# Attention of a gated cross-attention and mixture-of-experts layer: scores in pairs on two row strips, the row maximum as a bias, a new issue order

## The reference

```python
# x, ctx: 16 x 128 x 512 and 16 x 128 x 256; regrouped by 128 tokens
xn = (x - mean(x)) / sqrt(var(x) + 1e-5)
q = rope(xn @ Wq); k = rope(ctx @ Wk); v = ctx @ Wv          # 32 heads of 16
w = softmax(q @ k.T * 0.25, axis=-1)                          # per head, 128 x 128
x = x + tanh(g0) * ((w @ v) @ Wout + bout)
xn2 = (x - mean(x)) / sqrt(var(x) + 1e-5)
probs = softmax(xn2 @ gate_w.T); top 6
x = x + tanh(g1) * (sum over top 6 of probs * expert(xn2) + shared(xn2))
```

## Time and profile before

| | us |
|---|---|
| median of 3 runs | 1501.24 (1496.4 to 1513.0) |
| the profiled execution, its own time | 1500.2 |
| its span, first to last instruction | 1498.0 |

### The profile page before, as it was taken

One profiled execution on the slowest core, in us unless ns is written; L12 is line 12 of the kernel. 1 busy time (PEld: TensorE's weight loads), 2 busy tenths in 40 slices (PEclk: granted clock), 3 DMA queues, 4 the chain that ended last, 5 costly groups with the idle time before them and its releaser, 6 DMA issues.

```text
span 1498.0 us, 32482 instructions
## 1 busy us (share of the span) xinstructions
PE 1408.3 (94%) x8414; PEld 1187.6 (79%) x8415; DVE 839.9 (56%) x1682; ACT 499.7 (33%) x982; POOL 700.7 (47%) x1135
## 2 busy tenths in 40 slices
PE   4899999999999955999999999999999999999998
PEld 2566666666666644899999999999999999898987
DVE  4677777778777743444444444444444444256666
ACT  3344444445444411233333333333333333111111
POOL 3457754444544241548354555555555400745553
PEclk8799999999999856999999999999999999999999
DMA  5022323211321225534444444444443442356674
GB/s 190 18 92 76 134 92 134 75 75 75 119 105 65 79 108 178 168 100 141 144 141 144 141 144 141 143 143 143 143 143 107 122 143 86 104 166 202 206 206 138
DMA packets 146857, 190.03 MB, mean 127 GB/s; under 512 B 32531, under 2 KB 99604, under 8 KB 144116
## 3 DMA queue, kind: packets, MB, share of 16 engines
q1 hardware_dynamic: 125108, 99.31, 22.3%
q0 software_dynamic: 21696, 90.06, 17.5%
HBM read 116.80 MB, written 72.50 MB: 126 GB/s over the span
## 4 chain that ended last, share of the span: by engine, by line
PE 73%; DVE 13%; issue 5%; ACT 3%; SPq 2%; POOL 1%; DMA 1%; DVEq 0%; ACTq 0%; POOLq 0%
PE bank L1362 33%; PE bank L1396 18%; PE bank L616 8%; PE bank L641 5%; DVE smax L888 3%; PE bank L1373 3%; PE bank L654 2%; DVE soft L891 2%; PE bank L623 2%; PE bank L671 1%; ACT soft_t L533 1%; SPq L1183 1%; DVE x L937 1%; ACT soft L527 1%; DVE stats L940 1%
## 5 line engine op out<-in xcount | busy, mean ns | idle before, releaser
L1362 PE MATMUL bank<-w_hi,x_hi 128*128 (+1 forms) x1144 | 289.6, 334 | 21.0 <-DVE x_lo L1437 18.5
L1362 PE MATMUL bank<-w_hi,x_lo 128*128 (+1 forms) x1144 | 277.2, 323 | 0.0
L1362 PE MATMUL bank<-w_lo,x_hi 128*128 (+1 forms) x1144 | 276.9, 323 | 0.0
L205 POOL CAST w_hi<-w_raw 128x352 fp32r<-128x352 f32 x144 | 69.2, 531 | 379.2 <-PE bank L1362 379.2
L1453 DVE SCALAR_TENSOR_TENSOR act<-silu,row_w,bank 128x352 f32<-128x352 f32 x111 | 64.4, 580 | 301.2 <-ACT silu L1311 300.3
L1362 PEld LDWEIGHTS bank<-w_hi,x_hi 128*128 128x128 f32 x1144 | 193.0, 190 | 21.3 <-issue 18.6
L1311 ACT ACTIVATE silu<-bank 128x352 f32<-128x352 f32 x143 | 66.5, 465 | 402.7 <-PE bank L1362 402.7
L1362 PEld LDWEIGHTS bank<-w_lo,x_hi 128*128 128x128 f32 x1144 | 200.2, 189 | 0.0
L1362 PEld LDWEIGHTS bank<-w_hi,x_lo 128*128 128x128 f32 x1144 | 199.6, 189 | 0.0
L1396 PE MATMUL bank<-w_hi,a_hi 128*128 (+3 forms) x429 | 171.4, 400 | 7.6 <-DVE a_lo L1441 6.9
L1396 PE MATMUL bank<-w_lo,a_hi 128*128 (+3 forms) x429 | 169.7, 396 | 0.0
(11 more groups left out here) (183 smaller groups left out, 2316.8 us busy)
## 6 DMA issues: line engine op xcount, KB each, us to landing
xr<-expert_rows SPq DMA_DIRECT2D x444, 64.0 KB, 1.9
y_rows<-y SPq DMA_DIRECT2D x111, 256.0 KB, 2.0
w_raw<-in_w POOLq DMA_DIRECT2D x18, 1408.0 KB, 6.7
w_raw<-in_w POOLq DMA_DIRECT2D x18, 512.0 KB, 7.8
x_sb<-in_x SPq DMA_DIRECT2D x16, 256.0 KB, 3.0
x_res<-in_x SPq DMA_DIRECT2D x16, 256.0 KB, 3.9
x_rows<-x SPq DMA_DIRECT2D x16, 256.0 KB, 4.3
x_rows<-row SPq DMA_DIRECT2D x16, 256.0 KB, 4.4
```

The source lines that it names most:

```text
L205: nc.gpsimd.tensor_copy(w1_hi[d][half][:, s], w1_raw[:, d, halves[half]]).then_inc(w_hi_made, 1)
L1362: last = nc.tensor.matmul(to[:, 0:WIDTH], xx[jt][:, d, :], w[d][half][:, cols], start=(d == 0 and xx is x_hi and w is w1_hi), stop=(d == D ...
```

## The change

- PE issues the scores of two units together at even u, alternating between the two strips (`score_pair`), and waits for the exponentials of the unit just before (`exp_done` of u - 1 and older).
- DVE's maximum is written negated; the subtraction is gone. ACT reads the scores from PSUM and takes the exponential of each head with that maximum as the bias, four instructions per unit. The scale 0.25 moves into the masks of k (`C_EVEN`, `C_ODD`).
- The transposes of the rotated q go from u 4 to u 3 and of k from u 5 to u 4, with ACT's q_t copy from u 5 to u 3 and the k_t copies from u 5 to u 4.
- The output projection is issued in two halves, six matmuls at u 3 and six at u 4 behind the pair of scores. The addition of the bias and the residual go to u 5, the normalised row to u 7.
- `transpose_row` and `x2_hi` move to u 0 of PLACE, `c_hi` to u 0 and `c_lo` to u 1 of PROJECT, the router's chain from u 5 to u 3, the first statistics from u 2 to u 3, xn from u 6 to u 7. `rank` waits in addition for the projection to be read out of bank 1.
- SP issues the load of x before it waits for `c_lo`.
- `rsqrt` starts from a power of -0.5 on POOL and makes one Newton step instead of three.

```diff
@@ rsqrt, POOL
                 ch = Chain(pool, chain_sem, 2 + 3 * NEWTON, b)
+                if isinstance(b, int) and b == 0:
+                    pool.wait_ge(small_in, 16 * 5)
...
-                ch.step(g.tensor_scalar(y[:].bitcast(I32), vpos[:].bitcast(I32), -0.5, RSQRT_BITS, ALU.mult, ALU.add))
+                ch.step(g.tensor_tensor(y[:], vpos[:], const[:, C_HALF:C_HALF + 1], ALU.pow))
@@ attend, ACT
-                    act.wait_ge(shifted, b * GROUPS + u + 1)
-                    a.activation(soft[u % 2][:], soft[u % 2][:], ACT.Exp, scale=SCALE).then_inc(exp_done, 1)
+                    act.wait_ge(smax_done, b * GROUPS + u + 1)
+                    need(act, prob_mm, b * GROUPS + u - 1)
+                    for h in range(4):
+                        last = a.activation(soft[u % 2][:, h, :], bank[2 + u % 2][:, h * P:(h + 1) * P], ACT.Exp,
+                                            bias=smax[u % 2][:, h:h + 1])
+                    last.then_inc(exp_done, 1)
@@ score_pair, PE
-                    need(pe, shifted, b * GROUPS + u - 1)
+                    need(pe, exp_done, b * GROUPS + u)
                     for c in range(2):
+                        for w in (u, u + 1):
+                            r, ch = 32 * (w % 4), 2 * (w // 4) + c
+                            last = nc.tensor.matmul(bank[2 + w % 2][:, c * 2 * P:(c + 1) * 2 * P],
+                                                    q_t[j][r:r + 32, ch, :],
+                                                    k_t[j][r:r + 32, ch].rearrange("p e n -> p (e n)"),
+                                                    start=True, stop=True)
@@ one_round, PE
-                    scores(at, u)
...
+                    if u % 2 == 0:
+                        score_pair(at, u)
+                    if at(TAIL) and u == 4:
+                        project_out(1, *at(TAIL))
+                    if at(PROJECT) and u in (0, 4, 7):
+                        project(u, *at(PROJECT))
                         project_late(u, *at(PROJECT))
+                    if at(PLACE) and u == 0:
+                        transpose_row(*at(PLACE))
+                    probs(at, u)
+                    if at(TAIL) and u in (0, 2):
                         tail(u, *at(TAIL))
+                    if at(PROJECT) and u in (1, 2):
                         project(u, *at(PROJECT))
...
                     values(at, u)
+                    if at(PROJECT) and u == 3:
+                        project(u, *at(PROJECT))
                     if at(PLACE) and u == 6:
-                        rank(at(PLACE)[0])
+                        rank(at(PLACE)[0], at(TAIL))
                     if at(TAIL) and u == 3:
-                        project_out(*at(TAIL))
+                        project_out(0, *at(TAIL))
@@ attend, DVE
-                v.tensor_reduce(smax[u % 2][:], s3, AX.X, ALU.max).then_inc(smax_done, 1)
-                dve.wait_ge(smax_done, b * GROUPS + u + 1)
-                need(dve, prob_mm, b * GROUPS + u - 1)
-                v.tensor_tensor(soft[u % 2][:], s3, smax[u % 2][:, :, None].to_broadcast([P, 4, P]), ALU.subtract)\
-                    .then_inc(shifted, 1)
+                v.tensor_reduce(smax[u % 2][:], s3, AX.X, ALU.max, negate=True).then_inc(smax_done, 1)
@@ one_round, SP
                     waits_apart(sp, passed_sp, (xn_done, b - 1))
-                    waits_apart(sp, passed_sp, (c_lo_done, b))
                     if not (isinstance(b, int) and b == 0):
                         sp.dma_start(x_sb[j][:], x[b]).then_inc(x_in[j], 16)
+                    waits_apart(sp, passed_sp, (c_lo_done, b))
```

More of the change, by code:

```diff
@@ L563, in one_round @@
                     attend(at, u)
-                    if at(PROJECT) and u == 5:
+                    if at(PLACE) and u == 0:
+                        b = at(PLACE)[0]
+                        act.wait_ge(x2_mm, b + 1)
+                        need(act, gate_mm, b)
+                        a.activation(x2_hi[:].rearrange("p c n -> p (c n)"), bank[1][:], ACT.Copy)\
+                            .then_inc(x2_hi_done, 1)
+                    if at(PROJECT) and u == 0:
+                        b = at(PROJECT)[0]
+                        act.wait_ge(c_in, 16 * (b + 1))
+                        need(act, v_mm, b)
+                        a.activation(c_hi[:], c_raw[:], ACT.Copy).then_inc(c_hi_done, 1)
+                    if at(PROJECT) and u == 4:
                         b, j, n = at(PROJECT)
@@ L628, in _, with score_pair @@
             pe.wait_ge(ones_done, 2)
-            def scores(at, u):
+            def score_pair(at, u):
                 if at(ATTEND):
@@ L635, in scores @@
                         pe.wait_ge(kt_done, 2 * (b + 1))
-                    r = 32 * (u % 4)
-                    need(pe, shifted, b * GROUPS + u - 1)
+                    need(pe, exp_done, b * GROUPS + u)
                     for c in range(2):
[L640 to L645, removed]
+                        for w in (u, u + 1):
[4 more added lines that the diff above has]
+                                                    start=True, stop=True)
+                            if c == 1:
+                                last.then_inc(score_mm, 1)
             def probs(at, u):
@@ L717, in transpose_values, with project_out @@
                 four_transposes(bank[1], attn[:].rearrange("p h d -> p (h d)")).then_inc(at_mm, 1)
-            def project_out(b, j, n):
-                if isinstance(b, int) and b == 0:
-                    pe.wait_ge(w_lo_done, 3)
-                pe.wait_ge(at_lo_done, b + 1)
-                three(bank[1][:], at_parts, o_w, DC, lambda t, c: t[:, c, :], lambda w, c: w[:, c, :])\
-                    .then_inc(o_mm, 1)
+            def project_out(half, b, j, n):
+                if half == 0:
+                    if isinstance(b, int) and b == 0:
+                        pe.wait_ge(w_lo_done, 3)
+                    pe.wait_ge(at_lo_done, b + 1)
+                for c in (2 * half, 2 * half + 1):
+                    for l, r in ((0, 0), (0, 1), (1, 0)):
+                        last = nc.tensor.matmul(bank[1][:], at_parts[l][:, c, :], o_w[r][:, c, :],
+                                                start=(c == 0 and l == 0 and r == 0), stop=(c == DC - 1 and l == 1))
+                if half == 1:
+                    last.then_inc(o_mm, 1)
             def transpose_row(b, j, n):
@@ L739, in gate_logits, with rank @@
                 last.then_inc(gate_mm, 1)
-            def rank(b):
+            def rank(b, tail_at):
+                if tail_at:
+                    pe.wait_ge(chain_tail, TAIL_STEPS * tail_at[0] + 5)
                 pe.wait_ge(mask_done, b + 1)
@@ L858, in load @@
                 if u == 7:
-                    dve.wait_ge(c_hi_done, b + 1)
-                    need(dve, v_mm, b)
-                    v.tensor_tensor(c_lo[:], c_raw[:], c_hi[:].bitcast(F32), ALU.subtract).then_inc(c_lo_done, 1)
-                if u == 6:
                     dve.wait_ge(var1, b + 1)
@@ L876, in project @@
                 if u == 1:
+                    dve.wait_ge(c_hi_done, b + 1)
+                    v.tensor_tensor(c_lo[:], c_raw[:], c_hi[:].bitcast(F32), ALU.subtract).then_inc(c_lo_done, 1)
                     dve.wait_ge(q_mm, b + 1)
@@ L1051, in one_round @@
                 for u in range(GROUPS):
-                    if at(TAIL) and u in (3, 4):
+                    if at(TAIL) and u == 3:
                         tail(u, *at(TAIL), ch)
```

61 lines of the change are left out of this document (19 added, 42 removed).

## The result

The changed kernel runs at 1,497.7 us (median of 20 runs), the kernel before, run beside it, at 1,505.6 (20 runs). The ratio is 0.9948 [0.9924, 0.9972]: 0.5% faster. Applied to the 1,501.24 of the forecast it is 1,493.4, where 1,488 was forecast. The profiled execution took 1,490.3 (span 1,488.5), 9.5 less in span than the 1,498.0 before; the forecast had 12.9 less. Single executions of the changed kernel lie between 1,487.1 and 1,508.6. They go with the granted clock: mean clock 0.952 in the fastest, 0.927 in the slowest.

A forecast was written before the change was run, and what follows sets the result against it. TensorE was taken to bound each phase A round. 14 full rounds at 0.35 gave 4.9, plus 8 at the ends, 12.9 us off 1500.2: 1487.3, forecast as 1488 against the median, range 1464 to 1512.

The forecast's parts named there:

- the pair: Scores on TensorE: two units on two strips take 1.06 us together, saving 4.2 us of PE work per round.
- the column strips' 0.35: Attention times V: eight records on four column strips take 0.35 us together, a third of the serial price.
- the new wait: Pairs on TensorE wait for the preceding unit's exponentials: 3.65 us standing per round, giving 28.75 us.
- the clock falls: Middle rounds of phase A: fall to 1.2 GHz in 85 of 100, mean cost 1.6 us, round 30.4.
- rounds 5 and 6, rounds 3 and 4: Counted among the 14 full rounds, each gaining 0.35 us; 0.7 together.
- the transposes moved up: With row and c_hi moved a round: no cost beyond the laid-out order, covered by the wide work before them.
- the ends: Rounds 2 and 17 gain 3 and 4 us, plus the root's 1.8, less 0.8 for the drain: 8 in all.
- The root's 1.8: GpSimd's shorter root chain: gain 1.8 us in the last rounds, where the row waits for rstd.
- The power: The power on GpSimd that starts the root: taken as 0.3 us, bounds 0.2 and 1.0.
- "faster": Time below the no-change band of 1486.2 to 1516.3 us; chance 0.46.
- "same": Time within 1%, 1486.2 to 1516.3 us; chance 0.37.

The follow-up runs named there:

- kt_later: Changed kernel with ScalarE's two k_t copies moved from ahead of unit 5's exponentials to behind them; 1,450.7 us, ratio 0.9611.
- split_late: Changed kernel with GpSimd's splitting of the second expert's weights put into rounds 16 and 17; 1,488.5 us, ratio 0.986.
- kt_split: Changed kernel with both the k_t copies behind unit 5's exponentials and the second expert's weight splitting in rounds 16 and 17; 1,439.1 us, ratio 0.9551.
- clo_back: Changed kernel with c_hi and c_lo put back where the kernel before had them, unit 7 of LOAD; 1,498.3 us, ratio 0.9924.
- kt_clo: Changed kernel with k_t copies behind unit 5's exponentials and c_hi, c_lo back at their old place, splitting unmoved; 1,448.4 us, ratio 0.9621.
- old_root: Kernel with later k_t copies and late splitting, given the old root (bit seed, three Newton steps); 1,436.1 us against 1,436.8.
- same_strip: Changed kernel with both units of a pair on the even unit's strip, bank alternation kept; 1,579.6 us, ratio 1.0454.
- unpaired: Changed kernel issuing one unit's scores at a time, behind the exponentials of two units before; 1,509.3 us, ratio 1.0032.
- fill: Changed kernel with unread wide matmuls where TensorE stood, 8 before pair (6,7) and 4 before pair (0,1); 1,478.2 us, ratio 0.9806.
- kt_split_again: Changed kernel with later k_t copies and splitting in rounds 16 and 17, the same kernel run on another chip; 1,436.8 us, ratio 0.9558.

## Why the prediction was right or wrong

**Right: the pair.** 1.06, inside bounds of 0.9 and 2.12. The mark it was read by (the column strips' 0.35) held for row strips. The Trainium skill ("TensorEngine Tiling (Array Packing)", Key Properties) says that tiles work in parallel, and the 1.99 on one strip against 1.13 on two agree.

**Right: the new wait and its places.** PE stands for soft ahead of pair (6,7) and of pair (0,1): 1.60 and 0.83 (0.94 where the clock holds), laid out as 1.85 and 1.05. A round at clock 1.00 is 28.1, laid out as 28.75. The work was 25.17 for 25.1; the stands were sized 0.65 too long, in part by the exps. The group by line:

```profile
L532 ACT ACTIVATE soft<-bank,smax 128x128 f32<-128x128 f32 x412 | 117.4, 372 | 77.9 <-DVE smax L899 77.9
```

0.372 us each for 0.385; four come to 1.14, and ACT starts what follows after 1.00 (255.60 to 256.60 on its timeline), not 1.2. That the k_t copies were on this path stood in the layout as +1.15, and `kt_later` measured 1.15.

**Right: the clock falls.** Forecast in 85 of 100 rounds; of rounds 7 to 16, two kept it (28.07 and 28.14), two lost a little (29.4, 29.2), six took 30.8 to 32.7. It cost 2.2 a round in the place of 1.6. The two errors, +0.65 and -0.6, cancelled: the round was 30.28 for the forecast 30.4, the gain 0.42 for 0.35. The hit on the round is partly luck.

**Wrong: rounds 5 and 6.** The step that failed is one sentence: the transposes moved up, and row and c_hi a round on, were costed at nothing, "nothing but the order laid out above; their cover is the wide work before them". It was checked against a round of the middle, but rounds 5 and 6 are not like it: POOL has 10.6 and 5.7 us of weight splitting there, ahead of its q sums. The layout had no queue for POOL in those rounds. They lost 7.4 where 0.7 was forecast to be gained: 8.1 of the sum. `split_late` and `kt_split` show that the splitting is the cause (rounds 5 and 6 fall by 11.5 and 14.6 us when it goes), `clo_back` and `kt_clo` that c_lo's stretch is the smaller harm. That the larger one is the q transposes' earlier place is argued, from the stand of 4.75, and not tested by itself. The Trainium skill has a rule that speaks against this move ("SBUF — State Buffer", SBUF: two separate sides): a VectorE instruction with two SBUF inputs and a GpSimd instruction that reads SBUF exclude each other, each for the length of the other. c_lo is of that kind, and the rows agree in kind. In size they don't: c_lo lasted over some 13 of POOL's instructions in a row (9.46 us, of 0.43 and 0.89 each), and in `kt_later` over all 16 (10.71 us).

**Mis-sized: rounds 3 and 4.** They lost 2.1 where a gain of 0.7 was forecast. Here the mechanism is the forecast's own: the clock fell in both, and it cost 2.6 and 2.5 (29.35 and 30.63 for 26.8 and 28.1) in the place of 1.6 in the mean, 1.9 in a round that falls.

**Mis-sized: the ends.** 11.3 (3.4 + 7.9) for 8. The root's 1.8 in it is not borne out: `old_root` costs nothing that can be measured. By elimination the drain's gain would be the pairs' and the order's, but the drain of one kernel differs by 3 us between profiles, and no run separates them. The power took 0.57 us, for 0.3 inside 0.2 to 1.0 (the 1.0 was called the longest row on POOL; its subtractions of 128x512 are longer, three in 3.92), and the chain at the end of the stage 2.2 for 1.7 (541.68 to 543.88; 3.5 before).

**The total.** 4.2 + 3.4 + 7.9 - 9.5 = 6.0 at the first expert matmul. Phase B, whose code is the same, took another 3.5 less in this pair of profiles, at a clock of 1.00 for 0.99; that is not the change's. The medians differ by 7.8, half of the way to 1%. The time fell inside the range, but the chances leaned the wrong way: "faster" held 0.46, "same" 0.37. With the splitting out of the way the forecast's ratio of 0.991 lies inside what was measured (`split_late`, 0.986 [0.9802, 0.9918]).

**What the prediction did not see** is how near the better kernel was. The clock's fall and the k_t copies were both in the layout, as two terms. That taking 1.15 us of copies off the path also gives back the clock, 3.3 us a round in all, needed the two to be put together.

## What to carry to other kernels

When an edit moves a step, earlier or later, check it against each peeled or special round as well, and against every engine that has extra work there: here two moves that cost nothing visible in ten rounds lost more in two (7.4 us) than the ten gained (4.2). A wait costs TensorE twice, by standing and by the clock that falls behind it; so look for the one copy or conversion that sits between two activations on the path, and move that before anything larger. Where work is taken from TensorE, ask what will keep it busy in the place where the work was.

## What the runs showed of the hardware

- Eight fp32 score records on two row strips take 1.13 us, and the next record starts after 1.06. On one strip it is 1.99 and 1.92 (`same_strip`).
- Beside GpSimd's casts and two-input subtractions a VectorE subtraction between SBUF tiles took 9.46 us (128x256, 0.41 alone), 10.71 in `kt_later`: it got hardly anything until the splitting ended. In `clo_back` VectorE's work beside the subtractions (132.99 to 140.16) that reads PSUM kept its time. A product of 16 columns that reads only SBUF took 2.54, for 0.23 in the changed kernel (149.05), though the reciprocal of one column just ahead of it, SBUF alone too, took its 0.15:
```profile
136.03 0.68 DVE L862 TENSOR_TENSOR k_sin<-bank,sincos 128x512 f32<-128x512 f32 x1
...
137.67 0.68 DVE L901 TENSOR_REDUCE smax<-bank 128x4 f32<-128x512 f32 x1
138.27 0.15 DVE L972 RECIPROCAL grec<-gsum 128x1 f32<-128x1 f32 x1
138.45 2.54 DVE L974 TENSOR_SCALAR prob<-gexp,grec 128x16 f32<-128x16 f32 x1
```
- The clock fell behind a stand of 1.6 us (changed kernel), and also with PE busy 5.70 of 5.70 us on scores, transposes and V (`unpaired`). It held with stands of 0.44 and 0.94 (`kt_later`), with fillers (`fill`), and in some rounds behind the same stand of 1.6 (28.07 and 28.14 in the changed kernel). What the chip asks for is not settled by these runs.
- A power of 128x1 on GpSimd takes 0.57 us, three times a product of that size (0.19).
- The spread between runs of one kernel goes with the clock: 1,487 at 0.952 and 1,509 at 0.927. `kt_split_again` and `kt_split`, whose clock holds, spread over 8 and 11 us (6 runs each), the changed kernel over 21 (20 runs).
